# Five edits and a new instruction order in a fused convolution, attention and expert kernel

## The reference

```python
# layer 0: split-attention convolution
x = group_norm(hidden_state, 32)
x = silu(conv2d(x, w0, b0))                      # 1x1, 64 -> 64
x = group_norm(x, 16)
x = silu(conv2d(x, w1, b1, padding=1, groups=4)) # 3x3, 64 -> 128
x = group_norm(x, 2)
y = x.reshape(B, C, 2, 2, 8, 2, 8)               # two radix halves, four windows of 8x8
a = y.mean(axis=(4, 6)).max(axis=2)
a = conv2d(group_norm(silu(conv2d(a, w2, b2, groups=2)), 8), w3, b3, groups=2)
a = softmax(a.reshape(B, C, 2, 2, 2), axis=2)
out = group_norm(einsum('BCRHhWw,BCRHW,Cc->BcHhWw', y, a, weight), 32)
x = hidden_state + out
# layer 1, on tokens t (16 images, 256 pixels, 64 channels)
Q = tanh(ln(t) @ fc_w.T + fc_b);  e = Q @ score_w
t = t + causal_attend(ln(t), e)                  # online softmax over the 16 images, per pixel
h = relu(bn1(ln(t) @ W1[e] + b1));  h = relu(bn2(h @ W2[e] + b2))   # 8 experts
t = t + sum_e softmax(mean_over_images(ln(t)) @ Wr + br)[e] * (h @ Wo[e] + bo[e])
```

## Time and profile before

| what | us |
|---|---|
| three executions, median (lowest, highest) | 162.06 (161.11, 162.81) |
| the profiled execution, its own time | 162.24 |
| its span, first to last instruction | 160.4 |
| PE busy in the span | 138.7 |
| DVE busy | 100.5 |
| ACT busy | 77.0 |

### The profile page before, as it was taken

The page is one execution under the profiler, slowest core; times in us unless marked ns, Lnnn a source line. Parts: engine busy times, 40 slices in busy tenths (PEclk is TensorE's granted clock), DMA queues, the critical chain, the costliest instruction groups (busy, mean ns, idle before and its releaser), DMA issues.

```text
span 160.4 us, 2711 instructions
## 1 busy us (share of the span) xinstructions
PE 138.7 (86%) x1001; PEld 62.1 (39%) x1001; DVE 100.5 (63%) x384; ACT 77.0 (48%) x131; POOL 31.0 (19%) x27
## 2 busy tenths in 40 slices
...
DMA packets 3740, 4.63 MB, mean 29 GB/s; under 512 B 208, under 2 KB 3408, under 8 KB 3600
## 3 DMA queue, kind: packets, MB, share of 16 engines
...
q10 hardware_dynamic: 144, 0.20, 0.6%
...
...
## 4 chain that ended last, share of the span: by engine, by line
PE 61%; DVE 19%; ACT 10%; issue 3%; DMA 2%; POOL 2%; DVEq 0%; ACTq 0%
PE bank L805 10%; PE bank L954 9%; PE bank L929 8%; PE bank L942 7%; PE bank L770 4%; PE bank L763 3%; DMA xin<-x 2%; PE bank L822 2%; PE bank L847 2%; ACT h L400 2%; PE bank L855 2%; DVE ctxs L671 2%; PE bank L750 2%; ACT x L358 2%; PE bank L841 2%
## 5 line engine op out<-in xcount | busy, mean ns | idle before, releaser
L400 ACT ACTIVATE h<-bank,s_bnb,s_bns 128x512 f32<-128x512 f32 x32 | 23.2, 779 | 7.5 <-PE bank L929 7.4
L770 PE MATMUL bank<-warm 128*128 128x512 bf16 x80 | 21.0, 401 | 1.1 <-ACT y L337 1.1
L929 PE MATMUL bank<-xs,par 64*64 64x512 f32 x128 | 17.3, 611 | 1.4 <-ACT h L400 1.4
L805 PE MATMUL bank<-pad,w 32*64 32x512 f32 x288 | 17.0, 593 | 0.4 <-DVE pad L504 0.4
L942 PE MATMUL bank<-h,f2s 64*64 64x512 f32 x128 | 17.0, 602 | 0.2
L337 ACT ACTIVATE y<-bank,par 128x512 f32<-128x512 f32 x8 | 4.8, 688 | 21.0 <-PE bank L805 21.0
L763 PE MATMUL bank<-warm 128*128 128x512 bf16 x32 | 10.9, 487 | 1.3 <-POOL warm L304 1.3
L770 PEld LDWEIGHTS bank<-warm 128*128 128x128 bf16 x80 | 7.8, 106 | 9.9 <-issue 3.1
L805 PEld LDWEIGHTS bank<-pad,w 32*64 32x64 f32 x288 | 7.3, 130 | 7.4 <-issue 5.9
L547 DVE BATCH_NORM_STATS2 s_ws<-y 128x6 f32<-128x64 f32 x64 | 8.8, 209 | 0.3 <-ACT y L337 0.2
L329 ACT ACT_TABLE_LOAD x1 | 1.3, 1283 | 13.9 <-PE bank L776 13.9
...
## 6 DMA issues: line engine op xcount, KB each, us to landing
...
row_par<-row_params SPq DMA_DIRECT2D x2, 160.0 KB, 8.7
...
```

The source lines that it names most:

```text
L400: A.activation(h1[(2 * m + h) % 4][:], bank[Z1[h]][:], ACT.Relu, bias=tile("bnb", P, 3 * EP)[:, col:col + 1], scale=tile("bns", P, 3 * EP) ...
L770: T.matmul(bank[Z1[0]][:], warm[:, 0:P], warm[:], start=True, stop=True)
L805: ins = T.matmul(bank[CONV1[k][2 * j + h]][at:at + C, :], w1[rows, tap, :], pad[rows, b:b + 2, dy:dy + S, dx:dx + S], start=(tap == 0), st ...
L929: ins = T.matmul(bank[Z1[h]][to, :], f1[own, e, to], xs[own, k, q], start=True, stop=True)
```

## The change

Five edits to the steps, and a new `ORDER`:

1. *Raw moments to PE.* The statistics of `gn1`, `gn2`, `gn4` end on DVE with the BN_STATS and one instruction that squares the means; the sums over the halves are made on PE by four small products in place of one.
2. *Window sums.* `ws` sums each 8x8 window over two axes with one TENSOR_REDUCE for two images on DVE; the sums of squares are made on ACT, by two squares of 128x256 with a sum output. Three of the small steps of `gn3` go. The two images of a `silu` now lie side by side in y.
3. *Scale of the first expert layer in its weights.* ACT makes eight diagonal matrices (`spr`), PE a row of scales from them (`s1row`), DVE multiplies the weights. The relu has no scale operand.
4. *Part of that relu on DVE.* For m = 0 to 9 the second of the two relus is DVE's (`d1`).
5. *Context added early.* `t2` transposes into a bank of its own, and DVE adds it to x1; the output bank is started by the product with `bo`.

```diff
+        ON_DVE = {(m, 1) for m in range(10)}
...
+            def square_sums(u):
+
+                act.wait_ge(y_ready, u + 1)
+                k, s = u // 4, 2 * (u % 4)
+                for i in range(2):
+                    A.activation(more[:, u, i * PIX:(i + 1) * PIX], y[:, 2 * u + i, :], ACT.Square,
+                                 accum_out=tile(f"wsum{k}", P, 2, BK)[:, 1, s + i:s + i + 1]).then_inc(y_squared, 1)
...
+            def spread_first_scales():
+
+                act.wait_ge(scales_folded, 1)
+                for v in range(2):
+                    for e in range(EP):
+                        A.activation(spread1[:, v, e, :], w("ident"), ACT.Copy,
+                                     scale=tile("bns", P, 3 * EP)[:, v * EP + e:v * EP + e + 1]).then_inc(spread1_ready, 1)
...
                 for h in range(2):
-                    col = h * EP + e
-                    A.activation(h1[(2 * m + h) % 4][:], bank[Z1[h]][:], ACT.Relu, bias=tile("bnb", P, 3 * EP)[:, col:col + 1],
-                                 scale=tile("bns", P, 3 * EP)[:, col:col + 1]).then_inc(h1_ready, 1)
+                    if (m, h) not in ON_DVE:
+                        col = h * EP + e
+                        A.activation(h1[(2 * m + h) % 4][:], bank[Z1[h]][:], ACT.Relu,
+                                     bias=tile("bnb", P, 3 * EP)[:, col:col + 1]).then_inc(h1_ready, 1)
...
             def channel_stats(name, source, n, arrived=None):
...
                     ins = V.bn_stats(raw[:, i, :], source(i))
-                step(ins)
-                for i in range(n):
-                    ins = V.bn_aggr(mv[:, i, :], raw[:, i, :])
-                step(ins)
-                V.tensor_copy(e2[:, 0, :], mv[:, :, 0])
-                step(V.tensor_tensor(e2[:, 1, :], mv[:, :, 0], mv[:, :, 0], ALU.mult))
-                V.tensor_tensor(e2[:, 1, :], e2[:, 1, :], mv[:, :, 1], ALU.add).then_inc(stats_ready, 1)
+                ins.then_inc(moments_ready, 1)
+                dve.wait_ge(moments_ready, MOMENTS_AT[name])
+                means = raw.rearrange("p n (a t) -> p n a t", a=2)[:, :, :, 1]
+                V.scalar_tensor_tensor(sq, means, float(HALF_PIX), means, ALU.mult, ALU.mult).then_inc(stats_ready, 1)
...
             def window_stats(u):
                 dve.wait_ge(y_ready, u + 1)
-                k, j, h = u // 4, (u // 2) % 2, u % 2
-                ws = tile(f"ws{k}", P, BK * WIN, 6)
-                for i in range(2):
-                    b = 2 * (2 * j + i) + h
-                    img = y[:, k * BK + b, :].rearrange("p (a y c x) -> p a y c x", a=2, y=8, c=2)
-                    for n in range(WIN):
-                        ins = V.bn_stats(ws[:, b * WIN + n, :], img[:, n // 2, :, n % 2, :])
+                s = 2 * (u % 4)
+                ins = V.tensor_reduce(tile(f"wst{u // 4}", P, BK * WIN)[:, s * WIN:(s + 2) * WIN],
+                                      y[:, 2 * u:2 * u + 2, :].rearrange("p s (a y c x) -> p (s a) c y x", a=2, y=8, c=2), AX_XY, ALU.add)
                 step(ins)
...
+            def add_context(n):
+
+                dve.wait_ge(ctx_turned, n + 1)
+                dve.wait_ge(centred2, n + 1)
+                pairs, pixels = halves(n // Q, n % Q)
+                t = x1[:, pairs, pixels]
+                V.tensor_tensor(t, t, bank[TURN][:].rearrange("p (b n) -> p b n", b=PK), ALU.add).then_inc(ctx_added, 1)
...
+            def relu1(m):
+                if (m, 1) in ON_DVE:
+                    dve.wait_ge(z1_done, m + 1)
+                    if m >= 2:
+                        dve.wait_ge(z2_done, m - 1)
+                    col = EP + units[2 * m][2]
+                    V.tensor_scalar(h1[(2 * m + 1) % 4][:], bank[Z1[1]][:], tile("bnb", P, 3 * EP)[:, col:col + 1], 0.0,
+                                    ALU.add, ALU.max).then_inc(h1_by_dve, 1)
...
+            def moments_product(name, matrix):
...
+                pe.wait_ge(moments_ready, MOMENTS_AT[name])
+                for a in range(2):
+                    T.matmul(bank[SMALL][:, 0:2 * n].rearrange("p (t n) -> p t n", t=2), matrix, raw[:, a, 1:3, :], start=(a == 0), stop=False)
+                pe.wait_ge(stats_ready, STATS_AT[name])
+                for a in range(2):
+                    ins = T.matmul(bank[SMALL][:, n:2 * n], matrix, sq[:, a, :], start=False, stop=(a == 1))
+                ins.then_inc(small_ready, 1)
...
+            def first_scale_rows():
+
+                small(("s1row", 0))
+                pe.wait_ge(ones_ready, 1)
+                pe.wait_ge(spread1_ready, 2 * EP)
+                for v in range(2):
+                    ins = T.matmul(bank[SMALL][v * C:(v + 1) * C, :], ones[:], spread1[:, v].rearrange("p e m -> p (e m)"),
+                                   start=True, stop=True)
+                ins.then_inc(small_ready, 1)
...
                 for i in range(PK):
                     pe.wait_ge(ctx_ready, context_at(k, q, 2 * i + 1))
-                    T.matmul(bank[OUT[k][q]][:, i * P:(i + 1) * P], pair_of(ctxs, k, q, i), w("ident"), is_transpose=True,
-                             start=(i == 0), stop=False)
+                    ins = T.transpose(bank[TURN][:, i * P:(i + 1) * P], pair_of(ctxs, k, q, i), w("ident"))
+                ins.then_inc(ctx_turned, 1)
...
-                        T.matmul(bank[OUT[s][q]][:], r_("bo", s)[:, q * P:(q + 1) * P], turned, start=False, stop=False)
+                        T.matmul(bank[OUT[s][q]][:], r_("bo", s)[:, q * P:(q + 1) * P], turned, start=True, stop=False)
```

Of the new `ORDER` one line (the `heat` stages are 40 before and 12 now; the `warm` stages are 16 in both):

```diff
-    31 w3.1 gnaf.1 cen.1 att.0 wan.1 scan.0 gate.2 gate.3 heat.32 ynorm.3 ln2.0 ln2.1 outp.1 heat.33 heat.34 heat.35 gn4.1 xn2.0
+    cen.1 ynorm.3 ln2.0 gate.2 w3.1 gate.3 ln2.1 outp.1 xn2.0 xt.0 heat.11 gn4.1 xn2.1 gn4f.1 d1.0 l1.0 xt.1 x1.1 t2.0 l1.1 d1.1 l2.0
```

More of the change, by code:

```diff
@@ L31 @@
 PIX = S * S
+HALF_PIX = PIX // 2
 PAIRS = B // 2
@@ L71 @@
-    heat.4 ynorm.1 heat.5 heat.6 ws.6 heat.7 w3.0 gnaf.0 heat.8 heat.9 ws.7 wan.0 heat.10 heat.11 gate.0 heat.12 gate.1 outp.0 heat.13
-    heat.14 gn4.0 heat.15 heat.16 gn4f.0 heat.17 gn3.1 heat.18 x1.0 heat.19 tok.0 heat.20 gn3f.1 heat.21 ln1.0 heat.22 ln1.1 heat.23
-    heat.24 heat.25 win.1 hn.0 heat.26 ynorm.2 hch.0 heat.27 hn.1 w2.1 hch.1 fc.0 fc.1 score.0 heat.28 gna.1 cen.0 heat.29 coef.0 heat.30
-    heat.31 w3.1 gnaf.1 cen.1 att.0 wan.1 scan.0 gate.2 gate.3 heat.32 ynorm.3 ln2.0 ln2.1 outp.1 heat.33 heat.34 heat.35 gn4.1 xn2.0
```

139 lines of the change are left out of this document (79 added, 60 removed).

## The result

The changed kernel takes 161.11 us (median of 20 executions, 159.40 to 163.65) where the kernel before takes 162.06 (median of 20). The ratio is 0.9938, with a 95% interval of 0.9914 to 0.9962: faster by 0.6%, inside the 1% that the prediction called no change. The forecast was 160.0 us, 1.3% faster. Ratios and their intervals are taken over the fast executions of each kernel, medians in us over all of them. The profiled execution has a span of 159.4 us and a mean granted clock of 0.925; before it was 160.4 and 0.989.

The account below looks back on a forecast made before the run. PE alone bounds the convolution and the last stage, a chain over all engines the stretch between. Terms -1.75, +1.45, 0, -0.15, -1.2, -0.6 sum to -2.25 from 162.24: 160.0 us; own range 158.5 to 161.5, overall 157.6 to 164.5.

Parts of the forecast that it names:

- Head: From the start to the convolution: earlier clock rise and shorter statistics start the convolution at 20.45 instead of 22.19, -1.75 us.
- a product gains only 0.15 on the path: Norm statistics: from the last BN_STATS to the copy takes 1.25 us instead of 1.42, despite 0.8 saved on DVE.
- Convolution: First convolution, ending at 40.8: extra PE products and waits, less two zero matmuls, add 1.45 us.
- the wait at gn3.0: In the convolution: DVE starts the gn3 sum only at 35.45, so PE waits 0.25 us.
- rival two: ACT's squares: each sum costs an extra instruction of 0.2 us, +2.1 in all, 162.1, no change; chance 0.15.
- Window branch: Convolution's end to the gate product: six squares fill ACT's slack, gate product still 9.4 us after, change 0.
- gn4.0 to l1.0: Gn4.0 through attention to the first expert product: -0.15 from product and gn3.1 order, -1.2 from l1.0 starting at 87.4.
- Rival one: After the convolution: the clock falls where zero matmuls went, costing 4.7 us, 164.7, slower; chance 0.18.
- zero and output products fill 6.1 to 14 after the convolution, so the level should be back for gn4: After the convolution: the argument that PE stays busy enough to restore the clock, given against Rival one.
- Expert stage: The PE-bound stage from l1.0 to the end: 1.2 us gained up to the last context add, 0.6 lost later, -0.6.
- a granted clock near 0.5 between 50 and 90: Sign listed as showing the forecast wrong: PE at its lower clock level between 50 and 90 us.
- a second instruction behind each square: Sign listed as showing the forecast wrong: ACT issuing another instruction after each square, which was expected to take 0.31 back to back.

Follow-up runs that it names:

- the control: The changed kernel run again, nothing altered, on the same chip as the first follow-up kernels: 160.94 us, 0.9957 of the kernel before.
- e5h_no_fold: Changed kernel with zero matmuls put back, but first-layer scales not folded into the weights and all 32 relus on ACT with a scale operand: 163.49 us, 1.0101.
- e6_heats_sq: Changed kernel with zero matmuls put back and six of ACT's squares moved behind the window branch's w3.0: 157.97 us, 0.9766 of the kernel before.
- e8_more_heats: Changed kernel with zero matmuls put back, six squares moved behind w3.0, and six more zero-matmul stages: 157.24 us, 0.9733 of the kernel before.
- e1_heats: Changed kernel with 26 zero-matmul stages added between the convolution and l1.0, all else the same: 158.96 us, 0.9832 of the kernel before.
- e9_heats_again: The same program as e1_heats, repeated unchanged on another chip: 158.73 us, 0.9816 of the kernel before.
- e10_order_alone: Program of e1_heats with old statistics, no scale folding, all relus on ACT and late contexts; new order and window sums stay: 166.95 us, 1.0339.

## Why the prediction was wrong

**Head**: right, -2.00 for -1.75, though single executions of the new head scatter from -1.35 to -2.45. The fourteen zero matmuls from 1.32 took 5.67 and so ended at 6.99 (forecast 6.9); in the control they took 4.54, so the level rose earlier there than the forecast's 6.3 to 7.7. From the last BN_STATS (14.17 + 1.41) to the copy (16.78) are 1.20 (forecast 1.25). The forecast's "a product gains only 0.15 on the path" holds for gn2.0. For gn1 it was the wrong measure: DVE's 0.8 us, called a relief, are in front of the first copy in its queue, and undoing the moments cost 0.8%, about 1.3 us.

**Convolution**: right in kind, mis-sized, +1.89 for +1.45. `s1row` took 1.08 (0.9 forecast). The wait for ACT's banks, inside the group from 30.29, is 1.0, where the kernel before already hid 0.5 (96 instructions from 32.02 in 5.95 us instead of 5.42): 0.5 was added, not 0.2. The two zero matmuls gave back 0.44, not 0.6, and the wait at gn3.0 (0.25) hardly came. `e5h_no_fold` shows that `s1row` and this wait aren't two costs that add: without `s1row` the wait is 2.0 and the convolution as long. The squares are rival two's mechanism. ACT's timeline of the changed kernel:

```profile
31.66 0.43 ACT L356 ACTIVATE more<-y 128x256 f32<-128x256 f32 x1
31.96 0.22 ACT L356 ACTIVATION_READ_ACCUMULATOR more<-y 128x1 f32 x1
32.06 0.43 ACT L356 ACTIVATE more<-y 128x256 f32<-128x256 f32 x1
```

Each square is followed by an accumulator read, and the pitch, from start to start, is 0.40, not 0.31. So what the Trainium skill says of DVE, in the place that the prediction cited ("VectorE: DVE Perf Modes", "Two Vector instructions with no wait between them"), this trace shows for ACT too. Yet rival two's price of 2.1 us did not come: the eight squares of the first half end at 34.96, when DVE has its f2s product (35.15, 0.69 long) and the gn3 sum still to do, and the gate product came 9.29 after the convolution. The squares behind the convolution do stand on the path: with six of them moved the gate product comes 0.9 us earlier (`e6_heats_sq`, `e8_more_heats`). The forecast had already let them fill ACT's slack and counted DVE's saving as nothing, so its 0 came out although each square took 0.40.

**Window branch**: right, -0.12 for 0.

**gn4.0 to l1.0**: the step that failed. The sum had -0.15 and -1.2 here and put the clock at nothing; measured was +0.87. Rival one, which describes it, got a chance of 0.18. The reason given against it, that "zero and output products fill 6.1 to 14 after the convolution, so the level should be back for gn4", was true for gn4.0 and false for tok.0: the level was back from 50.7 and fell again at 57.6, after 6.9 us in which PE was busy for 4.59. The reason looked at one place that the zero matmuls left, not at each. Rival one's price was 4.7; measured were 1.8 to 2.8 behind the gate, and its 1.0 in the expert stage did not come. In the whole kernel the zero matmuls of `e1_heats` bring 1.2% (2.0 us) against the control, and those of `e8_more_heats` with the moved squares 2.2% (3.6 us). The prediction let this rival decide "from about a third of that on", 1.6 us, and it did decide between "faster" and "the same", though not for slower: the expert stage gained a further 1.0 that no term had. So the 161.11 is as near to 160.0 as it is by luck: a loss of 2.2 us and a gain of 1.0, both missed, offset each other in part. Without the clock the reorder was worth what was forecast: from the gate product to l1.0 37.05 and 36.2 us in the two executions of this program (`e1_heats`, `e9_heats_again`), 36.76 by the forecast.

**Expert stage**: -1.6 for -0.6, the right way and too small. Undone one at a time, the relus on DVE are worth 2.5 us, the folded scale about 1.8, the early context 2.4 without the clock. PE's wait for ACT's relus fell only from 5.0 to 4.3 us. What fell more is PE's idle time up to xt.3: 0.7 us of 31.4, where the kernel before had 2.2 of 30.6, and contexts and xt.1 lie in it now. The three gains don't show as 6.7 against the kernel before, because the new order without them takes 76.5 us here (`e10_order_alone`) and the old one 71.8. Which term of the forecast's -0.6 was too small can't be told apart from this.

What the forecast's list named as a sign that it was wrong, a granted clock near 0.5 between 50 and 90 and a second instruction behind each square, both came.
